# ScalarE and GpSimd take over the feed-forward's residual add from VectorE

## The reference

```python
x = x + 0.5 * ffn(layernorm(x))
x = x + attention(layernorm(x))       # 16 heads of 8, ends in its own layernorm with gamma, beta
x = x + 0.5 * ffn(layernorm(x))
# ffn(x): h = [x, -x]; h = 2*relu(s0*(h @ W0)); h = 2*relu(s1*(h @ W1)); h = s2*(h @ W2)
# W0, W1, W2 are +1/-1 by a boolean; widths 256 -> 512 -> 512 -> 128
```

## Time and profile before

| | us |
|---|---|
| median of 3 runs (827.98 to 829.57) | 828.3 |
| the profiled execution | 827.32 |
| its span, first to last instruction | 825.5 |

### The profile page before, as it was taken

How to read it: one execution, slowest core, us unless ns; L and a number is a source line. 1 busy time by engine, 2 the same in 40 slices (tenths; PEclk the granted TensorE clock), 3 DMA queues, 4 the chain that set the end, 5 groups by cost and what they waited for, 6 DMA issues and landing times.

```text
span 825.5 us, 18461 instructions
## 1 busy us (share of the span) xinstructions
PE 715.6 (87%) x7258; PEld 330.3 (40%) x7258; DVE 640.2 (78%) x1228; ACT 507.7 (62%) x739; POOL 374.5 (45%) x663
## 2 busy tenths in 40 slices
PE   5668696999999999999999999999999997987767
PEld 2333243444443444444443444444444444342333
DVE  6558678798888989798888879798888877786343
ACT  3325566666666676666766667666667665675632
POOL 4540427355261827255362728264462626254250
PEclk9989698999999999999999999999999999999797
DMA  3011010100101010110101010100101010100000
GB/s 67 24 35 59 2 39 22 40 33 16 46 15 60 14 60 16 40 34 15 46 15 59 15 60 15 54 21 27 46 3 60 15 46 16 46 15 3 14 13 13
DMA packets 29508, 25.62 MB, mean 31 GB/s; under 512 B 4336, under 2 KB 29424, under 8 KB 29424
## 3 DMA queue, kind: packets, MB, share of 16 engines
q1 hardware_dynamic: 28992, 24.07, 9.3%
q10 hardware_dynamic: 432, 0.39, 0.1%
HBM read 5.05 MB, written 4.19 MB: 11 GB/s over the span
## 4 chain that ended last, share of the span: by engine, by line
PE 53%; DVE 29%; POOL 6%; ACT 6%; issue 5%; POOLq 0%; DVEq 0%; ACTq 0%
DVE row_max L1092 12%; PE ps_z L596 11%; PE ps_z L597 10%; PE ps_c L726 9%; DVE ffn_lo L1042 9%; PE ps_s L675 5%; ACT ffn_hi L833 4%; PE ps_m L649 4%; DVE ffn_bn L1019 2%; PE ps_z L580 2%; PE ps_z L586 2%; PE ps_m L738 2%; DVE q_lo L1083 1%; PE ps_m L660 1%; DVE ffn_lo L1045 1%
## 5 line engine op out<-in xcount | busy, mean ns | idle before, releaser
L1092 DVE TENSOR_REDUCE row_max<-ps_s 128x4 f32<-128x1024 f32 x256 | 311.5, 1217 | 37.5 <-PE ps_s L675 35.6
L866 ACT ACTIVATE probs<-ps_t,score_scale 128x1024 f32<-128x1024 f32 x256 | 284.3, 1110 | 76.7 <-PE ps_t L688 76.5
L833 ACT ACTIVATE ffn_hi<-ps_z 128x512 f16<-128x512 f32 x288 | 170.8, 593 | 151.9 <-PE ps_z L597 64.0
L1042 DVE SCALAR_TENSOR_TENSOR ffn_lo<-ps_z,ffn_hi 128x512 f16<-128x512 f32 x256 | 174.0, 684 | 72.3 <-ACT ffn_hi L833 69.0
L596 PE MATMUL ps_z<-ffn_hi,w 128*128 128x512 f16 x512 | 196.2, 383 | 5.3 <-DVE ffn_lo L1042 4.4
L597 PE MATMUL ps_z<-ffn_lo,w 128*128 128x512 f16 x512 | 195.0, 381 | 0.0
L726 PE MATMUL ps_c<-probs,v_cols 128*32 128x256 f32 x2048 | 134.2, 390 | 5.9 <-issue 5.9
L675 PE MATMUL ps_s<-k_rows,q_rows 32*128 32x256 f16 x1024 | 102.8, 279 | 29.9 <-DVE row_max L1092 26.9
L688 PE MATMUL ps_t<-q_rows,k_rows 32*128 32x256 f16 x1024 | 102.9, 280 | 4.6 <-ACT probs L866 4.5
L491 POOL TENSOR_TENSOR max_scaled<-row_max,max_unit 128x16 f32<-128x16 f32 x64 | 14.1, 221 | 168.2 <-DVE row_max L1092 168.2
L596 PEld LDWEIGHTS ps_z<-ffn_hi,w 128*128 128x128 f16 x512 | 49.9, 98 | 85.8 <-DVE ffn_lo L1042 26.0
(11 more groups left out here) (122 smaller groups left out, 968.2 us busy)
## 6 DMA issues: line engine op xcount, KB each, us to landing
x<-L_attn_x SPq DMA_DIRECT2D x16, 256.0 KB, 2.6
q_rows<-q_hi SPq DMA_DIRECT2D x32, 128.0 KB, 2.1
y<-x SPq DMA_DIRECT2D x16, 256.0 KB, 2.1
k_rows<-k_hi SPq DMA_DIRECT2D x30, 128.0 KB, 2.1
q_rows<-q_lo SPq DMA_DIRECT2D x16, 128.0 KB, 2.1
q_rows<-no_max SPq DMA_DIRECT2D x16, 128.0 KB, 2.1
k_rows<-k_lo SPq DMA_DIRECT2D x15, 128.0 KB, 2.1
q_rows<-max_rows SPq DMA_DIRECT2D x64, 8.0 KB
```

Of the source, the lines that this page charges most:

```text
L833: a_.activation(ffn_hi[:, use, :], ps_z[use % 2][:], ACT.Relu if use else ACT.Copy, scale=1.0 if use else XN_SCALE).then_inc(z_hi, 1)
L866: a_.activation(probs[n % PROBS][:, j:j + 2, :], ps_t[:], ACT.Exp, scale=score_scale[:, 0:1]).then_inc(s_exp, 1)
L1042: v.scalar_tensor_tensor(out=ffn_lo[:, use, :], in0=ps_z[use % 2][:], scalar=0.0, in1=ffn_hi[:, use, :], op0=ALU.max, op1=ALU.subtract).th ...
L1092: v.tensor_reduce(row_max[hb % 2][:].rearrange("p (a l) e -> p l a e", a=2)[:, j:j + 2, :, g % 2], ps_s[:].rearrange("p l (a k) -> p l a k ...
```

## The change

The residual step of 29 of the 32 feed-forwards is split. ACT copies the bank, scaled, into a new SBUF tile `ffn_y` (`ffn_scaled`), behind the exponential of the unit in which DVE did the step; that frees the bank. POOL then adds the block's input (`residual`) and signals the new semaphore `f_sum`. Feed-forwards 0, 1 and 31 stay on DVE. SP's `load_x` and `store_x3`, and DVE's statistics of x1, wait for `f_sum`. On POOL the add of a second feed-forward stands behind `split_max(t-1, 3)` and ahead of `att_norm(t+1)`, that of a first one between `split_max(t, 1)` and `split_max(t, 2)`.

```diff
 sp steps:
-                    sp.wait_ge(z_free, Z_USES * (second_ffn(t - 3) + 1))
+                    sp.wait_ge(f_sum, sums(second_ffn(t - 3)))
                     store_x3(start)
...
-                    sp.wait_ge(z_free, Z_USES * (it.ffn_b + 1))
+                    sp.wait_ge(f_sum, sums(it.ffn_b))
                     load_x(start)
 pool:
+            def residual(f, src, dst, stored=None, based=None):
+                pool.wait_ge(z_free, Z_USES * (f + 1))
+                if based is not None:
+                    pool.wait_ge(s_base, based)
+                if stored is not None:
+                    at_least(pool, s_out, 16 * stored)
+                g.tensor_tensor(dst[:], ffn_y[:], src[:], ALU.add).then_inc(f_sum, 1)
...
                     split_max(t - 1, 3)
+                if t >= 3:
+                    residual(second_ffn(t - 3), x2[1 - par], x3, stored=t - 3)
                 if it.prep:
                     att_norm(t + 1, 1 - par)
...
                     split_max(t, 1)
-                    if not it.own_contexts:
-                        split_max(t, 2)
+                if it.ffn_b is not None:
+                    residual(it.ffn_b, x0, x1[par], based=t + 1)
+                if it.cur and not it.own_contexts:
+                    split_max(t, 2)
...
                     ffn_norm(it.next_a, x2[1 - par])
+                if not it.cur:
+                    residual(it.ffn_a, x2[par], x3, stored=t - 2)
 act:
+            def ffn_scaled(f):
+                act.wait_ge(z_full, Z_USES * f + Z_USES)
+                at_least(act, f_sum, sums(f) - 1)
+                a_.activation(ffn_y[:].rearrange("p t d -> p (t d)"), ps_z[1][:], ACT.Copy,
+                              scale=ffn_scale[:, 0:1]).then_inc(z_free, 1)
...
                     for p in pairs:
                         exps(tile, p)
+                    if s == 0 and t >= 3:
+                        ffn_scaled(second_ffn(t - 3))
+                    for f, _, piece in ffn_work(it, s - 1):
+                        if piece == FFN_RESIDUAL:
+                            ffn_scaled(f)
 dve:
-                    if s == 0 and t - 1 >= 2:
-                        ffn_residual(second_ffn(t - 3), x2[1 - par], x3, stored=t - 3)
-                    for f, second, piece in ffn_work(it, s - 1):
-                        if second:
-                            ffn_piece(f, piece, x2[par], x3, stored=t - 2)
-                        else:
-                            ffn_piece(f, piece, x0, x1[par], based=t + 1)
+                    for f, _, piece in ffn_work(it, s - 1):
+                        ffn_low(f, piece)
```

More of the change, by code:

```diff
@@ L160, in macaron_layer @@
         ffn_xn = sb("ffn_xn", [P, TT, P])
+        ffn_y = sb("ffn_y", [P, TT, P])
         ffn_hi = sb("ffn_hi", [P, 9, TILE], F16)
@@ L220, in macaron_layer @@
         f_bn, f_mv, f_rs, f_xn = sem("ffn_bn_done"), sem("ffn_mv_done"), sem("ffn_rstd_steps"), sem("ffn_xn_done")
+        f_sum = sem("ffn_residual_added")
         z_full, z_hi, z_free = sem("z_full"), sem("z_hi_made"), sem("z_free")
@@ L248, in second_ffn, with sums @@
             return 2 * tile + 5 if tile <= T - 5 else T + tile
+        def sums(f):
+            return f - 1
         def full(t, r):
@@ L435, in steps @@
                     start = start_of(t - 2)
-                    sp.wait_ge(z_free, Z_USES * (it.ffn_a + 1))
+                    sp.wait_ge(f_sum, sums(it.ffn_a))
                     store_x3(start)
@@ L1046, in z_rest, with ffn_residual @@
                                            in1=ffn_hi[:, 0, :], op0=ALU.mult, op1=ALU.subtract).then_inc(z_free, 1)
-            def ffn_residual(f, src, dst, stored=None, based=None):
+            def ffn_residual(f, src, dst, stored=None):
                 dve.wait_ge(z_full, Z_USES * f + Z_USES)
-                if based is not None:
-                    dve.wait_ge(s_base, based)
                 if stored is not None:
@@ L1056, in ffn_residual, with ffn_low @@
                                        op0=ALU.mult, op1=ALU.add).then_inc(z_free, 1)
-            def ffn_piece(f, s, src, dst, stored=None, based=None):
+            def ffn_low(f, s):
                 if s == 0:
@@ L1064, in ffn_piece @@
                     z_rest(f, 5 + FFN_MID_DONE[s])
-                elif s == FFN_RESIDUAL:
-                    ffn_residual(f, src, dst, stored, based)
+            def ffn_piece(f, s, src, dst, stored=None):
+                ffn_low(f, s)
+                if s == FFN_RESIDUAL:
+                    ffn_residual(f, src, dst, stored)
             def att_stats(par, f):
                 dve.wait_ge(z_free, Z_USES * (f + 1))
+                at_least(dve, f_sum, sums(f))
                 stats(x1[par], att_bn, TT, a_bn)
```

## The result

| | before | changed |
|---|---|---|
| median, us | 828.73 (6 runs, 827.74 to 829.90) | 832.79 (6 runs, 831.01 to 834.84) |
| the profiled execution, us | 827.32 | 834.84 |
| its span, us | 825.5 | 833.0 |

The ratio is 1.0051, 95% interval 1.0035 to 1.0066: 4.2 us slower (2.9 to 5.5). The forecast was 834.1, with a range of 829.8 to 837.5; it was counted from the earlier median of 828.3, as 5.8 us more.

What follows compares the result with a forecast made beforehand. The chain of waits was taken as PE 53% and DVE 29%, with DVE's freed time worth 0. Costs of 2.5 + 1.5 + 1.25 + 0.26 + 0.3 = 5.8 us on the 828.3 median gave 834.1 us, range 829.8 to 837.5.

Steps and rivals of the forecast that it cites:

- SP's wait, iteration 0: SP's queue, iteration 0: load_x waits for the add, place_max behind it lands late for PE's unit 24; 2.5 us.
- SP's wait, iteration 1: SP's queue, iteration 1: load, spreads and place_max come later, PE waits at unit 24; 1.5 us.
- GpSimd's queue, iteration 14: POOL's unbroken queue in iteration 14: the add lands in front of the ffn_xn PE waits for; 1.25 us.
- GpSimd's queue, iteration 15: POOL in iteration 15: 0.99 us idle before the second feed-forward's layernorm absorbs part of the add; 0.26 us left.
- copy on ACT, iteration 16: ACT in iteration 16: exponentials alternate with PE without a gap for the copy; 0.3 us.
- full iterations: Full iterations: idle time behind DVE's residual, and slack on ACT, POOL and SP, make gain and cost 0 us.
- The copy and the add: Durations of the added operations: copy on ACT 0.69 us, add on POOL 1.27 us.
- the landing: Time from place_max's issue to its landing, iterations 0 and 1: taken as 2.1 us, bounds 2.0 and 2.45.
- rival C: Full iterations pay too, POOL's or SP's slack being less: 0.4 us in each of 12, 839 us; chance 0.10.

Runs made afterwards that it cites:

- 6: Kernel before, with VectorE's residual done twice, first into a scratch tile, at 23 places of the full iterations: 828.24 us, ratio 1.0000.
- 1: Changed kernel, with SP's load_x and its wait moved behind place_max(t, 1): 827.94 us, ratio 1.0013 against the kernel before.
- 3: Half of the change on the kernel before: only the first feed-forwards' residuals move to ACT and POOL: 832.56 us, ratio 1.0059.
- 7: Changed kernel, in iteration 0 alone place_max(0, 1) issued ahead of load_x, both still behind the wait for f_sum: one execution, 833.02 us.
- 4: Changed kernel, load_x behind place_max(t, 1); in iterations 14 and 15 the add behind split_max(t, 0), store_x3 behind place_max(t, 0): 829.2 us, 1.0009.
- 5: The changed kernel run again, unedited, against the kernel before: 833.26 us, ratio 1.0054 (1.0034 to 1.0075).
- 10: Changed kernel, load_x behind place_max(t, 1), adds of iterations 14 and 15 later on POOL, tail_base(14) behind split_max(t, 0): 826.19 us, ratio 0.9981.
- 2: Half of the change on the kernel before: only the second feed-forwards' residuals move to ACT and POOL: 828.71 us, ratio 1.0016.
- experiment 8: Kernel before, with POOL's tail_base of iteration 14 moved behind split_max(t, 0): 825.59 us, ratio 0.9969.
- 11: Kernel before with tail_base of iteration 14 behind split_max(t, 0), a second time: 825.12 us, ratio 0.9970.

## Why the prediction was right, and where its terms were off

| Step | forecast, us | shift in the profiled pair, us |
|---|---|---|
| SP's wait, iteration 0 | 2.5 | 2.9 |
| SP's wait, iteration 1 | 1.5 | 1.2 |
| GpSimd's queue, iteration 14 | 1.25 | 1.24 |
| GpSimd's queue, iteration 15 | 0.26 | 0.22 |
| copy on ACT, iteration 16 | 0.3 | 0.24 |
| full iterations | 0 | 0.5, in small steps |
| sum of the five places | 5.8 | 5.8 |

**VectorE's time is worth nothing in full iterations.** Right, and shown from both sides: taking it away lengthens the idle time, adding it again (6) costs nothing that can be measured.

**The copy and the add.** 0.69 and 1.27 us as read from `v_cols` and `xn_bv`; measured 0.69 and 1.274. The estimate of 1.12 us, which the prediction worked out from the Trainium skill's GPSIMD Engine Reference (side-by-side accounting), was too low here. Its rule (Engine selection), that such an add doesn't belong on GpSimd, is borne out by the two durations: 1.27 us for the add, against 0.73 us for VectorE's operation, which scales as well. With 0.15 us less at each of four places (iterations 0, 1, 14 and 15) the sum would be 0.6 us smaller, not 0.5. The longer duration decided one place of 29 in full (iteration 14) and part of three others.

**SP's wait.** Right in place and mechanism (1, 3 and 7 show it). The issue came as worked out: 83.75 plus the shift of 0.5 until then gives 84.2 to 84.3, measured 84.37. The term that was mis-sized is the landing, taken as 2.1 us in both places. It was 2.44 in iteration 0, which is the upper bound that the earlier trace rows had given, and 1.83 in iteration 1, where four spreads go between the load and it. So the lower bound of 2.0 us, taken from other DMAs to `q_rows`, was too high. That the errors of +0.4 and -0.3 us cancelled in the sum is luck.

**The full iterations have slack.** In iteration 8 the placement is issued at 448.05 and PE comes at 451.95, 2.1 us after it can have landed (1.83 us); forecast 1.9. On GpSimd `split_max(t, 0)` ends at 431.13 and PE comes at 432.77, 1.6 us later; forecast 1.4. Both slacks hold, so rival C is not what happened. The shift of 0.5 us comes mainly in two steps, of 0.23 us at unit 28 of iteration 4 and 0.21 at unit 28 of iteration 7. At the first, VectorE's four aggregations of `ffn_mv` take 0.62 us in place of 0.38 and wait for nothing that the profile shows; at the second it pauses 0.2 us behind them. Experiments 1, 4, 5, 7 and 10 have both steps, 3 has one of 0.35 us at the first place, 2 and the versions of the kernel before have none there. So they go with the first feed-forwards' half of the change, and their cause stays open.

**Iterations 14 to 16.** In iteration 14 the layernorm that PE waits for begins after an unbroken queue that is one add longer. PE's wait grew by 1.68 us, to 5.10 where the prediction says 4.7: 1.24 us is the add, and 0.44 us is that PE itself comes that much sooner, which the wait swallows. Timeline of POOL and PE, changed kernel:

```profile
696.10 1.29 POOL L499 TENSOR_TENSOR x<-ffn_y,x 128x512 f32<-128x512 f32 x1
...
706.46 1.08 PE L601 MATMUL ps_z<-ident,ffn_xn 128*128 128x128 f32 x4 [5.10 <-POOL ffn_xn L481]
```

In iteration 15 GpSimd no longer idles 0.99 us ahead of that layernorm; in iteration 16 the copy stands between two exponentials, as worked out from the earlier trace rows:

```profile
778.66 1.12 ACT L894 ACTIVATE probs<-ps_t,score_scale 128x1024 f32<-128x1024 f32 x1 [0.57 <-PE ps_t L709]
779.67 0.68 ACT L869 ACTIVATE ffn_y<-ps_z,ffn_scale 128x512 f32<-128x512 f32 x1
...
780.24 0.38 ACT L906 ACTIVATE ctx_t<-ps_c 128x256 f32<-128x256 f32 x1
780.51 1.12 ACT L894 ACTIVATE probs<-ps_t,score_scale 128x1024 f32<-128x1024 f32 x1
```

**What stays open.** The medians differ by about 4.2 us, the forecast is 5.8. The forecast lies above the interval of the first comparison (2.9 to 5.5) and inside that of the second (2.8 to 6.2). A gain of 1 us or so elsewhere isn't excluded, nor is it shown. The profiled pair differs by 7.5 us, and not all of that is the change's doing: 0.7 us lay in the prologue and 1.2 us between iterations 1 and 2. With the five places and the 0.5 us of the full iterations this makes 8.2 us. The rest comes back in iterations 15 and 16, where the shift rises by 0.9 us and falls by 0.8 and 0.7 us; the shift of experiment 6, which has nothing of the change, does nearly the same there (0.7 up, 0.9 and 0.7 down), so this is scatter, much of it in the one trace of the kernel before.

## What to carry to other kernels

Relieve an engine only where its name stands in the bracket of the wait that follows: 18.5 us of VectorE's busy time lay in front of waits for other engines and were worth nothing. When the last step of a buffer's use moves to a slower path, list what stands behind the DMA that waits for it in the same queue: the load was not urgent, the 8 KB placement behind it was, and its place in the queue alone decided 4.1 us by the traces and 3.2 by the ratios. The ends of a pipelined loop have none of its slack; the same queue position that hides 1.25 us in 11 full iterations costs all of it in iteration 14. A look there for what could stand later gave the only versions that beat the kernel before, with the change and without it.

## What the runs showed of the hardware

Here a small DMA issued 0.45 us behind a 256 KB load on the same queue lands 0.6 us later than one without a load ahead. From the issue of the 8 KB placement to the start of the matmul that waits for it in iteration 0: 2.44 us behind the load, 2.46 in the kernel of experiment 3, 1.82 with the load behind it (7, one trace). In iteration 1 it is 1.83 us; there the last of the spreads, a 128 KB copy within SBUF, is issued 0.65 us ahead (127.50) and didn't delay it. A second sign: the median time from issue to landing of the first spreads (`q_rows<-q_hi`) is 2.4 us in the four traces where the load stands directly ahead of them without a wait between (changed kernel, 3, 5, 7), and 2.1 us in the nine others. The Trainium skill's DMA: Bandwidth & Descriptors (Queues, rings and completion order) says that a DMA's completion signal lands only after every earlier write of the same DMA engine; the 0.6 us agree with it but don't show that this is the cause, and the copies within SBUF cause no such delay. The order of the kernel before was itself at this edge: when experiment 8 was run again (11), its profiled execution had, in iteration 0,

```profile
81.56 0.63 SPq L382 DMA_DIRECT2D q_rows<-max_rows  x1
...
84.10 0.28 PE L677 MATMUL ps_s<-k_rows,q_rows 32*128 32x256 f16 x2 [1.41 <-DMA q_rows<-max_rows]
```

2.54 us after its issue, and 0.07 us later than DVE would have let it (1.34 us in the earlier trace rows).

TensorE's clock adds to the scatter between executions. Both kernels have a stretch at the lower level (granted clock 0.50, 1.2 GHz) from the end of iteration 1 on. PE had little to do ahead of it: it was busy for 1.07 of 3 us in the kernel before (125 to 128) and for 0.90 of 4 us in the changed one (128 to 132). Windows of the kernel before and of the changed kernel, with the busy time of PE, PEld, DVE, ACT and POOL and then the granted clock:

```profile
128.00:134.00 6.00, 3.51 (x40) 2.03 (x40) 5.73 (x21) 3.39 (x5) 4.26 (x7) 0.50 0.01 1
```

```profile
134.00:142.00 8.00, 6.24 (x68) 3.29 (x64) 5.89 (x21) 3.93 (x4) 6.78 (x11) 0.50 0.02 3
```

In the kernel before the stretch goes from 128 to 135 us, in the changed one, which is 4.8 us behind by then, from 132 to 142, so it is some 3 us longer; the shift grows by 1.2 us there. That is no fixed price of the change: between the same points the changed kernel run again (5) lost 0.8 us, and experiment 3, which does the same work up to there and has as long a stretch (129 to 139), lost nothing. Whether the stalls make such a stretch longer stays open. The kernel of experiment 2 had a stretch of 10 us at the lower level in iteration 15 (744 to 754) that the kernel before has not, and its shift grew by 3.1 us there: its profiled execution took 832.61 us, its median is 828.71. So the time of one profiled pair can't stand for the two medians; the shift, event by event, tells where the two executions part.
